# Attention denominators: ten key blocks summed by GpSimd and six by one chain of accumulating DMAs, instead of nine and seven in two chains

## What is computed

```python
def _attention(q, k, v, bias):
    hd = q.shape[-1]
    scores = jnp.einsum('bhqd,bhkd->bhqk', q, k) / jnp.sqrt(jnp.float32(hd))
    if bias is not None:
        scores = scores + bias[None, None]
    attn = jax.nn.softmax(scores, axis=-1)
    return jnp.einsum('bhqk,bhkd->bhqd', attn, v)
...
out_short = _attention(q, k_s, v_s, decay_bias)
out_long = _attention(q, k_l, v_l, None)
out = alpha * out_short + (1.0 - alpha) * out_long
```

## Time and profile before

| | |
|---|---|
| median of 3 runs | 5284.13 us (5282.34 to 5284.47) |
| profiled execution, its own time | 5280.23 us |
| its span, first to last instruction | 5278.4 us |
| TensorE busy over the span | 95% |
| VectorE | 79% |
| ScalarE | 55% |
| GpSimd | 51% |
| granted TensorE clock, mean | 0.983 |

### The profile page before, as it was taken

One profiled execution on the slowest core, in us unless ns is written; L12 is line 12 of the kernel. 1 busy time (PEld: TensorE's weight loads), 2 busy tenths in 40 slices (PEclk: granted clock), 3 DMA queues, 4 the chain that ended last, 5 costly groups with the idle time before them and its releaser, 6 DMA issues. The chain is left out here.

```text
span 5278.4 us, 97228 instructions
## 1 busy us (share of the span) xinstructions
PE 5016.3 (95%) x27884; PEld 2067.5 (39%) x27884; DVE 4163.2 (79%) x7250; ACT 2899.9 (55%) x5206; POOL 2707.6 (51%) x988
## 2 busy tenths in 40 slices
PE   5998899999999999999999999999968999999999
PEld 2444233333333333333333333333315555555555
DVE  6556688888888888888888888888836777777776
ACT  2222167777767777677777777777653333333332
POOL 3000187888878788888878888787860000000000
PEclk8999799999999999999999999999988999999999
DMA  3443377767767776776777676777660000000000
GB/s 113 133 124 109 87 171 173 170 169 175 171 168 171 174 173 167 177 168 171 168 176 172 167 178 166 174 167 174 153 157 23 18 18 24 18 18 18 24 18 12
DMA packets 210097, 660.66 MB, mean 125 GB/s; under 512 B 25668, under 2 KB 105156, under 8 KB 152198
## 3 DMA queue, kind: packets, MB, share of 16 engines
q0 software_dynamic: 64512, 469.79, 38.3%
q1 hardware_dynamic: 145159, 185.65, 11.6%
HBM read 123.56 MB, written 61.64 MB: 35 GB/s over the span
## 5 line engine op out<-in xcount | busy, mean ns | idle before, releaser
L831 DVE TENSOR_REDUCE rowmax_parts<-scores_qk 128x1 f32<-128x512 f32 x4096 | 2523.1, 678 | 465.1 <-PE scores_qk L904 465.1
L811 ACT ACTIVATE probs_T<-scores_kq 128x512 f32<-128x512 f32 x4096 | 2286.3, 596 | 979.7 <-PE scores_kq L904 914.9
L745 POOL TENSOR_TENSOR probs_added<-probs_added,probs_T 128x2048 f32<-128x2048 f32 x448 | 2030.3, 4532 | 457.2 <-ACT probs_T L811 445.8
L904 PE MATMUL scores_kq<-q_operand,k_operand 103*128 103x512 f16 (+3 forms) x3712 | 1274.6, 349 | 11.0 <-ACT probs_T L811 9.1
L904 PE MATMUL scores_qk<-k_operand,q_operand 96*128 96x512 f16 (+4 forms) x3712 | 1123.1, 352 | 43.3 <-DMA k_operand<-positions_dram 19.7
L975 PE MATMUL outputs_T<-probs_T,v_operand 128*32 128x512 f32 x8192 | 1091.9, 605 | 1.3 <-ACT probs_T L811 1.3
L904 PEld LDWEIGHTS scores_kq<-q_operand,k_operand 103*128 103x128 f16 x3712 | 358.6, 97 | 921.8 <-ACT probs_T L811 636.6
L1423 PE MATMUL f_gate_up<-w_gate_up,xq_T 128*128 128x352 f32 x2048 | 627.2, 462 | 0.8 <-issue 0.8
L904 PEld LDWEIGHTS scores_qk<-k_operand,q_operand 96*128 96x128 f16 (+1 forms) x3712 | 354.8, 98 | 438.3 <-DVE rowmax_parts L831 184.3
L1423 PEld LDWEIGHTS f_gate_up<-w_gate_up,xq_T 128*128 128x128 f32 x2048 | 382.5, 190 | 202.1 <-issue 2.8
L745 POOL TENSOR_TENSOR probs_added<-probs_T 128x2048 f32<-128x2048 f32 x64 | 290.3, 4536 | 239.1 <-ACT probs_T L811 239.1
(11 more groups left out here) (155 smaller groups left out, 3938.2 us busy)
## 6 DMA issues: line engine op xcount, KB each, us to landing
probs_poured<-probs_T POOLq DMA_DIRECT2D x448, 1024.0 KB, 7.2
qk_parts_dram<-qk_parts SPq DMA_DIRECT2D x96, 256.0 KB, 2.6
q_operand<-qk_parts_dram SPq DMA_DIRECT2D x192, 128.0 KB, 2.6
k_operand<-qk_parts_dram SPq DMA_DIRECT2D x192, 128.0 KB, 3.2
v_dram<-v_heads SPq DMA_DIRECT2D x16, 1024.0 KB, 5.7
v_operand<-v_dram SPq DMA_DIRECT2D x64, 256.0 KB, 5.9
q_operand_above<-qk_parts_dram SPq DMA_DIRECT2D x96, 128.0 KB, 2.8
x_groups<-x SPq DMA_DIRECT2D x8, 1024.0 KB, 9.3
```

The costliest lines, as they stand in the source:

```text
L745: nc.gpsimd.tensor_tensor(total, first, probs[:, b % PBUF, :], ALU.add).then_inc(added.sem, 1)
L811: nc.scalar.activation(probs[:, kb % PBUF, qt * BANK:(qt + 1) * BANK], pb[:, k % 2, :], ACT.Exp)\
L831: nc.vector.reduce_max(rowmax[:, w % 2, c // NQ, c % NQ:c % NQ + 1], pa[:, k % 3, :], AX.X)\
L904: return nc.tensor.matmul(out, lhsT, rhs, start=start, stop=stop, skip_group_check=True)
```

## The change

Sums of 16 blocks are still formed for each unit, with other shares:

- GpSimd adds ten blocks (1, 2, 4, 5, 7, 8, 10, 11, 13, 14) with 9 instructions, one more than before.
- One chain of pours takes six blocks (0, 3, 6, 9, 12, 15), one pour fewer. The chain of every second unit has a destination array of its own (two arrays in turn, with a semaphore each).
- TensorE makes two count groups a unit: `probs_added` in step 1 of the next unit as before, `probs_poured` in step 4 of it. The group in step 14 is gone.
- `take_sums` stands in ScalarE's step 6 instead of 5, and the four inversions in VectorE's steps 6 to 9 instead of 5 to 8. `WEIGH` and `MIX` stay at 10 and 11.

```diff
--- before.py
+++ after.py
@@ -550,18 +550,18 @@
 ASTEPS = 10
 
 TURN_MAX = 10
-INVERT = 5
+INVERT = 6
 WEIGH = 10
 MIX = 11
 
 
-BY_POOL = (0, 1, 3, 5, 7, 9, 11, 13, 14)
-BY_DMA = ((2, 6, 10), (4, 8, 12, 15))
+BY_DMA = (0, 3, 6, 9, 12, 15)
+BY_POOL = tuple(b for b in range(KB) if b not in BY_DMA)
 ADDS = len(BY_POOL) - 1
-POURS = [len(blocks) for blocks in BY_DMA]
-COUNT_POURED = (14, KB + 3)
+POURS = len(BY_DMA)
 COUNT_ADDED = KB + 1
-TAKE_SUMS = 5
+COUNT_POURED = KB + 4
+TAKE_SUMS = 6
 
 
 def adds_until(kb):
@@ -596,7 +596,7 @@
         ones = sb("ones", [P, HD], F32)
         probs = sb("probs_T", [P, PBUF, L], F32)
         added_sum = sb("probs_added", [P, 2, L], F32)
-        poured_sum = [sb(f"probs_poured{i}", [P, L], F32) for i in range(2)]
+        poured_sum = sb("probs_poured", [P, 2, L], F32)
         rowmax = sb("rowmax_parts", [P, 2, KB, NQ], F32)
         negmax = sb("negmax", [P, 2, KB], F32)
         maxT = sb("negmax_T", [KB, 2, P], F16)
@@ -629,9 +629,9 @@
         expd = Rises(sem("a_exp"), UNITS * CHUNKS, credit=1)
         summed = Rises(sem("a_pv"), UNITS * KB, credit=1)
         added = Rises(sem("a_added"), UNITS * ADDS, credit=1)
-        poured = [Rises(sem(f"a_poured{i}"), UNITS * POURS[i], 16) for i in range(2)]
+        poured = [Rises(sem(f"a_poured{i}"), UNITS // 2 * POURS, 16) for i in range(2)]
         counted = Rises(sem("a_counted"), UNITS, credit=1)
-        counted_poured = [Rises(sem(f"a_counted_poured{i}"), UNITS, credit=1) for i in range(2)]
+        counted_poured = Rises(sem("a_counted_poured"), UNITS, credit=1)
         taken = Rises(sem("a_o_taken"), UNITS, credit=1)
         sums_out = Rises(sem("a_sums_out"), UNITS, credit=1)
         inverted = Rises(sem("a_inverted"), UNITS * NQ)
@@ -723,7 +723,7 @@
 
         @block.gpsimd
         def _(pool):
-            give_credit(pool, [maxed, expd, summed, added, counted, taken, sums_out, weighed] + counted_poured + stored)
+            give_credit(pool, [maxed, expd, summed, added, counted, taken, sums_out, weighed, counted_poured] + stored)
             nc.gpsimd.memset(ones[:, :], 1.0).then_inc(consts, 1)
             nc.gpsimd.memset(ident[:, :], 0.0).then_inc(chain, 1)
             pool.wait_ge(chain, 1)
@@ -736,33 +736,33 @@
 
                 total = added_sum[:, w % 2, :]
                 wait_apart(pool, expd, expd.at(n, (w * KB + b + 1) * NQ), passed)
-                if b == 1:
-                    first = probs[:, 0, :]
+                if b == BY_POOL[1]:
+                    first = probs[:, BY_POOL[0], :]
                     wait_apart(pool, counted, counted.at(n, w - 1), passed)
                 else:
                     first = total
                     wait_apart(pool, added, added.at(n, w * ADDS + adds_until(b) - 1), passed)
                 nc.gpsimd.tensor_tensor(total, first, probs[:, b % PBUF, :], ALU.add).then_inc(added.sem, 1)
 
-            def pour(w, n, b, c):
-
-                i = BY_DMA[c].index(b)
+            def pour(w, n, b):
+
+                i = BY_DMA.index(b)
+                total, landed = poured_sum[:, w % 2, :], poured[w % 2]
                 wait_apart(pool, expd, expd.at(n, (w * KB + b + 1) * NQ), passed)
                 if i == 0:
-                    wait_apart(pool, counted_poured[c], counted_poured[c].at(n, w), passed)
-                    nc.gpsimd.dma_start(poured_sum[c][:, :], probs[:, b % PBUF, :]).then_inc(poured[c].sem, 16)
+                    wait_apart(pool, counted_poured, counted_poured.at(n, w - 1), passed)
+                    nc.gpsimd.dma_start(total, probs[:, b % PBUF, :]).then_inc(landed.sem, 16)
                 else:
-                    wait_apart(pool, poured[c], poured[c].at(n, w * POURS[c] + i), passed)
-                    nc.gpsimd.dma_start(poured_sum[c][:, :], probs[:, b % PBUF, :], accum_op=ALU.add)\
-                        .then_inc(poured[c].sem, 16)
+                    wait_apart(pool, landed, landed.at(n, w // 2 * POURS + i), passed)
+                    nc.gpsimd.dma_start(total, probs[:, b % PBUF, :], accum_op=ALU.add).then_inc(landed.sem, 16)
 
             def one_pass(n):
                 for w in range(UNITS):
-                    for b in range(1, KB):
-                        if b in BY_POOL:
+                    for b in range(KB):
+                        if b in BY_DMA:
+                            pour(w, n, b)
+                        elif b != BY_POOL[0]:
                             add(w, n, b)
-                        else:
-                            pour(w, n, b, int(b in BY_DMA[1]))
 
             with nc.Fori(0, PASSES // 2, engines=[pool.engine], hint_back_edge=True) as m:
                 for i in range(2):
@@ -781,7 +781,7 @@
                 nc.scalar.copy(maxT[:, w % 2, :], pt[0:KB, 0:P]).then_inc(roundm.sem, 1)
 
             def take_sums(w, n):
-                act.wait_ge(counted_poured[1].sem, counted_poured[1].at(n, w + 1))
+                act.wait_ge(counted_poured.sem, counted_poured.at(n, w + 1))
                 act.wait_ge(weighed.sem, weighed.at(n, w))
                 nc.scalar.copy(sums[:, :], pc[:, :]).then_inc(sums_out.sem, 1)
 
@@ -803,8 +803,8 @@
                         if b in BY_POOL:
                             act.wait_ge(added.sem, added.at(n, u * ADDS + adds_until(b)))
                         elif u >= 0 or not first:
-                            c = int(b in BY_DMA[1])
-                            act.wait_ge(poured[c].sem, poured[c].at(n, u * POURS[c] + BY_DMA[c].index(b) + 1))
+                            landed = poured[u % 2]
+                            act.wait_ge(landed.sem, landed.at(n, u // 2 * POURS + BY_DMA.index(b) + 1))
                         for qt in range(NQ):
                             k = (w * KB + kb) * NQ + qt
                             act.wait_ge(scoredB.sem, scoredB.at(n, k + 1))
@@ -983,25 +983,24 @@
                                           start=first, stop=last)
                 mm.then_inc(done.sem, 1)
 
-            def count_poured(w, n, c):
-
-                if c == 0:
-                    pe.wait_ge(sums_out.sem, sums_out.at(n, w))
-                pe.wait_ge(poured[c].sem, poured[c].at(n, (w + 1) * POURS[c]))
-                count(poured_sum[c], counted_poured[c], c == 0, c == 1)
-
             def count_added(w, n):
 
+                pe.wait_ge(sums_out.sem, sums_out.at(n, w))
                 pe.wait_ge(added.sem, added.at(n, (w + 1) * ADDS))
-                count(added_sum[:, w % 2, :], counted, False, False)
+                count(added_sum[:, w % 2, :], counted, True, False)
+
+            def count_poured(w, n):
+
+                landed = poured[w % 2]
+                pe.wait_ge(landed.sem, landed.at(n, (w // 2 + 1) * POURS))
+                count(poured_sum[:, w % 2, :], counted_poured, False, True)
 
             def counts(w, n, i):
 
-                for c in range(2):
-                    if i == COUNT_POURED[c]:
-                        count_poured(w, n, c)
                 if i == COUNT_ADDED:
                     count_added(w, n)
+                if i == COUNT_POURED:
+                    count_poured(w, n)
 
             for c in range(CHUNKS):
                 scores_for_max(0, 0, c)
```

## The result

The changed kernel takes 5563.27 us in the median of 4 runs (5556.1 to 5563.58); the kernel before, on the same chip, 5283.24 us (5279.42 to 5284.47). The ratio is 1.0528, 95% interval 1.051 to 1.0546. The change costs 280 us. The forecast was 5352 us, in a range up to 5440: the direction was right, the size four times too small.

The account below looks back on a forecast made before the run. TensorE bounds the kernel before at 51.4 us a unit; GpSimd's loop of 10.0 + 0.6 + 41.8 = 52.4 us would replace it, adding 68 us to 5280.2, plus 3.9 to the median: 5352 us, range 5300 to 5440.

Parts of the forecast that it names:

- The count group: On TensorE: one count group less takes 0.86 us off a unit, 51.4 to 50.5 us.
- The copy queues behind the last accumulating pour: On the DMA engines at a unit's boundary: block 0's copy lands 2.7 us after block 15's accumulating pour.
- t + 10.0: Landing of the next unit's block 0 copy, 10.0 us after t, the issue of a unit's last pour (block 15).
- the 7.3 us for the last pour itself: On the DMA engines: block 15's pour lands 7.3 us after its issue, taken between 6.9 and 7.6.
- Four groups of a pour and two adds: On GpSimd, from block 3's pour to block 15's: four groups of 10.45 us, 41.8 us in all.
- GpSimd's loop as the bound: Pours and adds on GpSimd take 52.4 us a unit; TensorE waits 1.9 us a unit for the last add.
- the moved inversions: On VectorE, four of 0.94 us each, one step later: no cost while TensorE waits, else 0 to 0.2 us a unit.
- the slower rival: At a unit's end the last two pours run into the operand loads: loop 54.1 us, about 5459 us; chance 0.13.

Follow-up runs that it names:

- after_psum: The changed kernel with the inverses and the odd units' weighed outputs kept in the PSUM bank of the sums: 5318.76 us, ratio 1.0075 to the kernel before.
- mix_sbuf: As after_psum, but both weighed outputs go to SBUF and the mixing reads its two operands there: 5374.11 us, ratio 1.0176 to the kernel before.
- before_weigh11: The kernel before with the weighing in step 11 instead of 10 and the mixing in 12 instead of 11: 5730.09 us, ratio 1.085.

## Why the prediction was wrong

- **The count group** was right: 0.84 to 0.86 us a unit from the steps. Once nothing else is in the way a unit takes 50.6 us.
- **The copy queues behind the last accumulating pour**: right in kind. I had t + 10.0 after the last pour's issue. It landed 11.4 us after t in the median (the change and after_psum), 2.7 and 2.5 us behind the landing of the last pour: the copy's 2.7 us of DMA work were right. What was too small is the 7.3 us for the last pour itself, which landed after 8.4 (the change) and 8.1 (after_psum). The 7.6 that I had read is the median over all accumulating pours; those of block 15 took 8.6 in the kernel before too. Loads still run beside it: in the 12 us behind the last pour at 1807.10 in the changed kernel they took 27.1% of the engines' time, 3.3 us.
- **Four groups of a pour and two adds**: mis-sized, 41.8 us taken for what is 40.3 (median of after_psum). The 10.45 us were read as GpSimd's own time, "where the exponentials are ahead". They were not: the row of that add says `[0.43 <-ACT probs_T L811]`, and it started 0.35 us after the end of its block's exponentials, like all of its kind. Where the exponentials are there, an add starts 0.6 us after the issue of a pour (1783.18, 1783.78), and a group takes 1783.18 - 1773.08 = 10.1 us. With the later landing the two errors cancel by luck: 11.4 + 0.6 + 40.3 = 52.3 us, and after_psum measured 51.9 on average (median 52.4).
- **GpSimd's loop as the bound**: right only where the collision is taken away. In the change itself TensorE waited 2.6 us for the last add, not 118.
- **The step that failed** is the one on VectorE: "It costs nothing while TensorE waits 1.9 us a unit anyway". That was said of the moved inversions, and they did cost nothing (steps 6 to 9 take 3.2 us each, step 5 gives back 0.2). But it was all that the sum had for VectorE: the weighing behind them was no term of it, since I took every duration of VectorE as its own. The weighing's 742 ns held only as long as no add of GpSimd ran. GpSimd's ninth add and the new places of the pours moved the adds under it; the weighing itself had not moved a step. 3.1 us more a weighing on VectorE (3835 ns on average), and the lower clock after each stop of TensorE, are what the sum lacked: 5.4 us a unit in steps 10 to 13.
- **The row was there.** The line of the weighing had 741/742/4304 in the trace of before. An instruction that takes the same time 63 times of 64, and nearly six times as long once, depends on something that 63 times happens to be absent.
- **The range.** It was said to hold most of the slower rival, whose own time of 5459 us lies above its end of 5440. Neither was met, and the time came out above both by another mechanism.

By the Trainium skill, "SBUF — State Buffer", section "Who interferes with whom", a VectorE instruction with two SBUF inputs contends with a GpSimd instruction that reads SBUF, and whichever starts first makes the other block fully. The runs agree on who contends: 742 ns with no add running, up to 5.7 us with one; the copy out of PSUM (690 ns) and the inversion (940 ns), each with one input, kept their time in the changed kernel, with an add running beside nearly all of them. Both sides can be held up: in mix_sbuf two adds whose rows begin 0.01 and 0.04 us behind that of a mixing took 5.06 and 5.03 us instead of 4.53. But the order of the rows doesn't always tell who goes first: five weighings of the changed kernel begin 0.12 to 0.40 us ahead of an add and still waited for the end of it. This was a rule that spoke against the change, and I had not weighed it.

## What to carry to other kernels

Before a change fills up an engine, look which instructions of its neighbours run in its gaps, and what they would take without the gap. An outlier in a duration's maximum is the place to look. In a periodic schedule a lucky phase is invisible: all units show the same good value, and an edit that moves a phase can lose it. Moving one operand to PSUM makes the instruction independent of the phase and costs nothing here (ratio 1.0001). And of two transfers in one queue, the one that something waits for should be issued first. Last, a median over all instructions of a line can hide the one kind that a sum needs: the last pour of a unit landed 1 us later than the median of its line.

## What was not expected of the hardware

- The wait for GpSimd shows as a longer instruction on VectorE, not as idle time: no list of waits names it, only the duration does.
- After TensorE had stood still for 3.35 us, the granted clock was 0.53 in the next 3 us; the mean over the span went from 0.983 to 0.959, and to 0.949 with the weighing and the mixing both caught (before_weigh11). The step behind the stall takes 4.6 us in the median instead of 3.0, so a stall of some 3.5 us costs about 1.6 us more.
- An accumulating 1 MB transfer holds the 16 DMA engines for twice as long as a copying one (5.2 and 2.7 us), and a copy issued 0.6 us behind it lands 2.5 to 2.7 us after it (medians), as if it had to wait for all of it.
- GpSimd issues a pour 0.57 us after the landing that it waited for (median, 63 of the 64 units of after_psum), and starts an add 0.35 us after the exponentials that it waited for (384 adds of the kernel before).
